# Seven of 28 pieces of the pooling of x folded by TensorE in the three steps without expert tiles

## The reference

```python
pooled = x.reshape(B, C, 14, 16, 14, 16).sum(axis=(3, 5))      # sums over 16x16 patches: 196 tokens an image
h = einsum('bcij,ce->bije', pooled, channel_weights)            # width 192
# attention, 12 heads of 16, weights 1 + qk + qk^2/2, relu, normalised by their sum
h = h + attention(layernorm(h)) @ w_proj + b_proj
# mixture of 8 experts (192 -> 768 -> 192, gelu), the best 2 of a softmax router, weighted
h = h + experts(layernorm(h))
```

## Time and profile before

| | us |
|---|---|
| runs | 1414.0, 1405.11, 1417.02; median 1414.0 |
| the profiled execution, its time | 1408.19 |
| its span, first to last instruction | 1406.3 |
| TensorE busy | 1232.2 (88%) |
| VectorE busy | 953.2 (68%) |
| sums of x (L1071), 448 of them | 358.2 |
| mean granted clock of TensorE | 0.935 of full |

### The profile page before, as it was taken

How to read it: one execution, slowest core, us unless ns; L and a number is a source line. 1 busy time by engine, 2 the same in 40 slices (tenths; PEclk the granted TensorE clock), 3 DMA queues, 4 the chain that set the end, 5 groups by cost and what they waited for, 6 DMA issues and landing times.

```text
span 1406.3 us, 26911 instructions
## 1 busy us (share of the span) xinstructions
PE 1232.2 (88%) x7299; PEld 1091.8 (78%) x7299; DVE 953.2 (68%) x3405; ACT 593.2 (42%) x1127; POOL 603.5 (43%) x485
## 2 busy tenths in 40 slices
PE   4766766789898989898989898989899889999986
PEld 3755655678787878788888888888888778888875
DVE  6799988487878787878787878787846223333444
ACT  0221224254544444444444444444444434454554
POOL 0004435414545445454545454545464553353332
PEclk9985557899999999999999999999999989999999
DMA  8679878568787878787878787777544654454554
GB/s 298 244 254 351 307 249 272 185 188 254 208 255 203 259 199 255 208 249 213 246 218 245 216 247 216 242 221 240 126 112 82 204 102 92 92 100 86 114 131 105
DMA packets 126505, 284.42 MB, mean 202 GB/s; under 512 B 24773, under 2 KB 70454, under 8 KB 126454
## 3 DMA queue, kind: packets, MB, share of 16 engines
q1 hardware_dynamic: 83350, 242.56, 52.3%
q0 software_dynamic: 43104, 41.25, 17.0%
HBM read 228.79 MB, written 54.95 MB: 202 GB/s over the span
## 4 chain that ended last, share of the span: by engine, by line
PE 28%; DMA 23%; POOL 17%; issue 15%; DVE 14%; ACT 2%; SPq 2%; POOLq 1%; DVEq 0%; ACTq 0%
DMA result<-ys,ridx 12%; PE ps L996 11%; PE ps L965 9%; POOL rows_d L616 9%; DMA rows_d<-rows,sloti 8%; POOL result L631 8%; DVE red L1071 5%; PE ps L805 2%; DMA w1r<-L_ffn_w 1%; PE ps L912 1%; DVE stats L1199 1%; DMA xr<-rows_d 1%; PE ps L1026 1%; SPq L484 1%; DVE topi L1208 1%
## 5 line engine op out<-in xcount | busy, mean ns | idle before, releaser
L631 POOL DMA_INDIRECT result<-ys,ridx x210 | 334.7, 1594 | 341.7 <-issue 189.8
L996 PE MATMUL ps<-w2a,hid 128*128 x2520 | 452.3, 327 | 1.8 <-ACT hid L730 1.8
L616 POOL DMA_INDIRECT rows_d<-rows,sloti x256 | 256.8, 1003 | 434.0 <-DMA rows_d<-rows,sloti 132.2
L996 PEld LDWEIGHTS ps<-w2a,hid 128*128 128x128 f32 x2520 | 415.2, 191 | 12.8 <-issue 3.0
L1071 DVE TENSOR_REDUCE red<-xbuf 128x21 f32<-128x672 f32 x448 | 358.2, 840 | 9.0 <-DMA xbuf<-x 8.0
L730 ACT ACTIVATE hid<-ps,b1s 128x512 f32<-128x512 f32 (+1 forms) x344 | 222.5, 653 | 264.2 <-PE ps L965 214.3
L965 PE MATMUL ps<-xh,w1h 128*128 128x512 f32 (+1 forms) x344 | 157.8, 459 | 21.7 <-ACT hid L730 8.1
L1308 DVE TENSOR_TENSOR xl<-ps,xh 128x512 fp32r<-128x512 f32 (+1 forms) x58 | 37.2, 641 | 200.8 <-ACT xh L749 200.8
L1331 DVE TENSOR_TENSOR w1l<-w1r,w1h 128x768 fp32r<-128x768 f32 x114 | 107.6, 949 | 45.8 <-ACT w1h L742 45.5
L965 PE MATMUL ps<-xl,w1h 128*128 128x512 f32 (+1 forms) x344 | 133.4, 388 | 0.0
L965 PE MATMUL ps<-xh,w1l 128*128 128x512 f32 (+1 forms) x344 | 133.3, 387 | 0.0
(11 more groups left out here) (165 smaller groups left out, 1584.3 us busy)
## 6 DMA issues: line engine op xcount, KB each, us to landing
xbuf<-x SPq DMA_DIRECT2D x224, 672.0 KB, 6.2
w1r<-L_ffn_w SPq DMA_DIRECT2D x118, 384.0 KB, 4.2
xr<-rows_d SPq DMA_DIRECT2D x48, 402.0 KB, 3.8
result<-h1s SPq DMA_DIRECT2D x32, 294.0 KB
w2a<-L_ffn_w SPq DMA_DIRECT2D x8, 576.0 KB, 7.2
rows_d<-rows,sloti POOLq DMA_INDIRECT x256
rows_d<-pad SPq DMA_DIRECT2D x9, 402.0 KB, 3.9
result<-ys,ridx POOLq DMA_INDIRECT x210
```

What stands on the lines that cost most here:

```text
L616: pool.indirect_dma_start(rows_d, bass.IndirectOffsetOnAxis(ap=sloti[:, k * NT + t:k * NT + t + 1], axis=0), rows[:, t, :], None).then_inc ...
L631: pool.indirect_dma_start(out, bass.IndirectOffsetOnAxis(ap=ridx[:, b, n:n + 1], axis=0), ys[:, b, n, :], None, compute_op=ALU.add).then_i ...
L996: last = mm(yout(g, b, n), hid[:, m % 3, cols], w, start=False, stop=m == MC - 1 and n % 2 == 1)
```

## The change

In steps 1, 2 and 3 the first seven half pieces are not summed by VectorE from `xbuf`. A new name `K.0` to `K.6` on TensorE multiplies each by the identity in four products of 128 x 168, one for each quarter (8 columns) of its 21 groups of 32, all accumulated in the same 168 columns of PSUM, three half pieces to a bank (banks 3, 4 and 5, unused in these steps). VectorE's `P` for these then sums 21 x 8 elements from PSUM; it waits for a whole bank of folded pieces at a time (`s_fold`): pieces 0 to 2 after `K.2`, 3 to 5 after `K.5`, 6 after `K.6`. The count `s_pooled`, which lets SyncE load the next chunks, is raised by VectorE as before. `K.0` to `K.4` stand ahead of `S3`, `K.5` and `K.6` between `S3` and `S4`. In steps 1 and 2 the names `P` are spread in another way: 16 instead of 18 stand ahead of `S6.0`, and one each behind `S6.0` and `S6.3` more. `LAST` keeps its places of `P`. The scatters' groups of six are as they were.

```diff
-STEP_ALONE = """S3 P P P P P P P P P P P P P P P P S4 S5 P P S6.0 S6.1 P S6.2 P S6.3 S7.0 P P S7.1 P P S8.0 P S8.1 P S8.2 P P S8.3
-    T1 S10 T2 R V.0 V.1 S11 V.2 V.3 S9 Q0 Q1 Q2 Q3""".split()
+STEP_ALONE = """K.0 K.1 K.2 K.3 K.4 S3 K.5 K.6 P P P P P P P P P P P P P P P S4 S5 P S6.0 P S6.1 P S6.2 P S6.3 P S7.0 P P S7.1 P P
+    S8.0 P S8.1 P S8.2 P P S8.3 T1 S10 T2 R V.0 V.1 S11 V.2 V.3 S9 Q0 Q1 Q2 Q3""".split()
-LAST = """S3 P P P P P P P P P P S4 S5 P P P G0 S6.0 S6.1 S6.2 S6.3 S7.0 P S7.1 P G4 P P S8.0 S8.1 S8.2 S8.3 S10
+LAST = """K.0 K.1 K.2 K.3 K.4 S3 K.5 K.6 P P P P P P P P P P S4 S5 P P P G0 S6.0 S6.1 S6.2 S6.3 S7.0 P S7.1 P G4 P P S8.0 S8.1 S8.2 S8.3 S10
...
+FOLDED = 7
+FOLD = EIGHTH // 4
...
+        s_fold = sem("pieces_folded")
...
+        def folded(p):
+
+            return ps[:, 3 + p // 3, p % 3 * SUMS * FOLD:(p % 3 + 1) * SUMS * FOLD].rearrange("q (n w) -> q n w", w=FOLD)
...
             lone[0] = not with_tiles and not last
+            by_pe[0] = not with_tiles
...
+            pe.sem_inc(s_fold, FOLDED)
+
+            def K(s, p):
+
+                k, h = p // HALVES, p % HALVES
+                pe.wait_ge(d_x[k % XSLOTS], (s + 1) * (16 * CHUNKS // XSLOTS) + 16 * (k // XSLOTS) + 16)
+                pe.wait_ge(s_pooled, s * PARTS + FOLDED)
+                for w in range(0, EIGHTH, FOLD):
+                    last = mm(folded(p), ident, xbuf[:, k % XSLOTS, h, :, w:w + FOLD], start=w == 0,
+                              stop=w == EIGHTH - FOLD)
+                last.then_inc(s_fold, 1)
...
             def P(s, p, first=False):
...
                 if p == 0 and not first:
                     dve.wait_ge(s_mix, s + 1)
-                if h == 0:
+                if by_pe[0] and after_first(s) and p < FOLDED:
+                    dve.wait_ge(s_fold, s * FOLDED + min(p // 3 * 3 + 3, FOLDED))
+                    V.tensor_reduce(red[:, p * SUMS:(p + 1) * SUMS], folded(p), AX.X, ALU.add).then_inc(s_pooled, 1)
+                    return
+                if h == 0 or p == FOLDED:
                     dve.wait_ge(d_x[k % XSLOTS], (s + 1) * (16 * CHUNKS // XSLOTS) + 16 * (k // XSLOTS) + 16)
```

More of the change, by code:

```diff
@@ L369, in vit_layer @@
         at_end = [False]
-        rank_bank, lone = [2], [False]
+        rank_bank, lone, by_pe = [2], [False], [False]
         def groups(j):
@@ L1037, in T1 @@
                 S1(s + 1)
-            schedule(pe, {"S1": S1, "T1": T1, "S3": later(S3), "S4": later(S4), "S5": S5, "S6": S6, "S7": S7, "S8": S8,
+            schedule(pe, {"S1": S1, "T1": T1, "K": later(K), "S3": later(S3), "S4": later(S4), "S5": S5, "S6": S6, "S7": S7, "S8": S8,
                           "S9": S9, "M": M, "X": X, "N": N, "G2": G2, "G3": G3})
```

## The result

Over 22 runs each, the changed kernel takes 1409.22 us (median; 1402.87 to 1414.56), the kernel before 1413.38 (1405.11 to 1421.65): a ratio of 0.9967, 95% interval 0.9953 to 0.9981, so 4.2 to 4.7 us faster. That is real and small: 0.3%. The profiled execution takes 1409.34 us, its span is 1407.5, its mean granted clock 0.939. The profile of before was a low draw of its kernel (1408.19), so the two spans can't be subtracted; I compare the lone steps inside them, of which before has this one trace. A run more than 1.5% above the fastest of its kernel counts as slow and stays out of the ratios: that takes away nine of the twelve runs of a variant further down (e5), its profiled one among them, and 13 of the 25 of the kernel before beside e1 to e4, so those ratios carry little and the medians of all runs stand beside them.

The account below looks back on a forecast made before the run. VectorE's sums of x were taken to bound steps 1 and 2, scatters and the w1 load step 3. Terms -1.3 and -2.6 made -3.9 us: 1407 from the mean, 1410 from the median, stated as 1408; range 1398 to 1420.

Parts of the forecast that it names:

- (c): Rival, whole kernel: the shift is absorbed by later scatters or waiting tiles, no effect, 1411 us; chance 0.18.
- (d): Rival, lone steps: full saving, S3 hardly late or step 3's idle time gone too, 7.8 less, 1403 us; chance 0.10.
- The work: Each lone step: 56 matrix instructions on TensorE, 0.14 us each at full clock; VectorE's short sums cost 0.26 us each.
- The clock: TensorE during K: low at the start, rising 4.1 us after K starts, between 2.7 and 5.4.
- (a): Rival, TensorE: the low clock holds through K and beyond, +21 us, 1432; chance 0.10.
- (b): Rival, TensorE: the clock rises late, at about 12 us, +2 us a step, 1415; chance 0.12.
- S3 late: TensorE: K.0 to K.4 ahead of S3 make it start 3.3 us late (2.8 to 4.0).
- The head: VectorE's sums ahead of S6: it comes for S6 at 114.2 instead of 117.29, 3.1 us earlier.
- The moved sums: Steps 1 and 2: two sums move behind S6, 1.53 us, idle time takes most of them, costing +0.5 us.
- The wait for the scatters: At S11 in step 1: step 0's scatters are through at about 141.7, so the step gives 1.3 us, not 2.6.
- Step 2: Its wait for scatters has 4.8 us to spare, so it gives 2.6 us.
- Step 3: Bound by scatters and the load of w1; its sums save nothing of their own.

Follow-up runs that it names:

- e5: The changed kernel with all of K moved behind T1 of the step before; median 1513.5 us (kernel before 1512.4), ratio 0.9923.
- e1: The kernel before with only the new places of P in steps 1 and 2; median 1511.7 us (kernel before 1509.7), ratio 1.0072.
- e4: The changed kernel without K in step 3; median 1510.5 us (kernel before 1509.7), ratio 1.0083.
- c1: The changed kernel again, no edit, on a faster chip; median 1404.8 us (kernel before 1415.3), ratio 0.9932.
- e2: The changed kernel with K run but VectorE still summing the long pieces; median 1509.0 us (kernel before 1509.7), ratio 1.0042.
- c0: The changed kernel again, no edit, on a slower chip; median 1512.6 us (kernel before 1512.4), ratio 0.9987.
- e9: The changed kernel with K.0 to K.2 behind T1 of the step before, and unused products filling two gaps; median 1411.8 us (kernel before 1415.3), ratio 0.9979.
- e3: The changed kernel with each product of K issued twice; median 1543.3 us (kernel before 1509.7), ratio 1.0270.
- e8: The changed kernel with three unused products in each gap before and after S5, steps 1 and 2; median 1408.2 us (kernel before 1415.3), ratio 0.9957.

## Why the prediction was right

The forecast was 1408, with -3.9 us as the sum; measured were 1409.22 and -4.2. Step by step:

- **The number.** The ratio's interval is -2.7 to -6.6 us. It holds the forecast's -3.9 and leaves out rivals (c), nothing, and (d), -7.8. That the level came out at 1408 as well is partly luck, since four runs with a spread of 12 us stood behind it.
- **The work.** 56 matrix instructions a step, in 7.80 + 2.47 us; the prediction had 7.65 + 2.24. At the full clock 16 take 2.40 from start to start, 0.15 each (0.14 predicted). Short sums take 0.33, 0.24 from start to start (0.33, 0.26).
- **The clock.** It rose 3.8 us after K began (2.7 to 5.4 predicted, 4.1 taken), in c1 at 99.9, 4.9 after. In all traces in which K stands ahead of S3 and begins at the low clock, 21 steps, it took 2.7 us (e2, step 2) to 5.3 (c0, step 3). The stay at the low clock, rival (a), and the late rise, (b), are out. By the Trainium skill, "TensorE: Matmul & The Clock Gate", Part 4, a transpose by the identity (in TensorE's transpose mode) does not count as activity. A plain product with the identity does, as these windows show. The Trainium skill, "TensorE: Matmul & The Clock Gate", Part 1, says that the number of products before the rise varies between executions of one kernel. The 3.8 and 4.9 us agree: 13 instructions of K had begun in the one, 17 in the other.
- **S3 late.** It starts 100.16 - 92.53 = 7.63 us after the ranking's end instead of 4.36: 3.3 late, as predicted. VectorE idles ahead of its fourth and its seventh sum (1.54, 0.33), as predicted.
- **The head.** -2.9 us in step 1 for -3.1 predicted, -3.4 in step 2. The step that I had wrong without harm: I took the clock as full through S6's first pair (113.2 against VectorE's 114.2, a margin of 1.0). It fell before S6, the pair took 1.69, and the margin was gone: TensorE came 0.1 after VectorE. In c0 and c1 the fall came before S5 and the gain shrank to 0.6 or 0.7 in one step each. So the right sum rests on a clock that falls late enough, and its range should have held that case: it is worth +2 us a step.
- **The moved sums.** I took +0.5 a step, since idle time should take most of them. Of the 1.01 us of idle time before, 0.84 are still there (0.26 and 0.58). From the first reciprocal to S11 step 1 takes 27.45 us instead of 25.70, 1.75 more; 0.26 of them are the wait at S11, so that 1.5 of the 1.53 stayed. In step 2, before idles twice:

```profile
169.33 0.36 DVE L1199 BATCH_NORM_STATS2 stats<-h1s 98x6 f32<-98x192 f32 x1 [1.02 <-ACT h1s L708]
171.78 0.36 DVE L1199 BATCH_NORM_STATS2 stats<-h1s 98x6 f32<-98x192 f32 x1 [0.95 <-ACT h1s L708]
```

  and from reciprocal to S11 it lost only 0.46 (27.16 for 26.70).
- **The wait for the scatters.** It is there (0.26 at 139.50) and ends 5.8 us after step 0's last scatter is issued at 133.71; I had 6.2, with an end at 141.7 for which the rows give only the last packets before 141. Step 1 gained 1.23 for the 1.3 of the cap. But the forecast had VectorE wait 1.3 there and it waited 0.26; what kept step 1 at 1.2 was mostly the moved sums. Two terms were off against each other: the right number came partly by the wrong one, and that is luck.
- **Step 2** gave 2.57 for 2.6, again by other parts: the head 3.4 shorter, from reciprocal to S11 0.46 longer, and VectorE's first sum 0.4 later against the scatters. **Step 3** gave 0.49 for 0. The first scatter of step 2 is at 183.06; with the 2.3 us added by which the setup was shorter it is 185.4 (185.3 predicted).
- **The rivals in the other runs.** Rival (c), nothing, is outside c1's interval too. c0's, 0.9949 to 1.0026, is wide enough to hold both (c) and the forecast. Rival (d), the full saving of 7.8, is against the distances, -4.3 in the first trace and 124.15 - 127.64 = -3.5 in c1; but c1's ratio, 0.9932 (4 runs against 19), would be -9.6 us, and its interval meets those of c0 and of the 22 runs at their ends only. Where the other 5 us of these four runs come from stays open; no distance in the lone steps shows them.

## What to carry to other kernels

Before work is moved to an idle engine, ask what else its idle time decides: here the added products, 10.0 us of them, filled 7.2 us of idle time and shortened the stages behind them by 5.2 with the clock that they raised, while the same products done earlier (e5, e9) left TensorE waiting for ScalarE, and the clock low behind that wait. When a change brings two engines level, as VectorE and TensorE at S6 here, more work on the one comes out in the time (e3: +8.6 us for +7.8), and small variations of a clock show at once. An effect of 0.3% in a kernel whose executions spread by 1% is read from distances within the changed part, not from two spans.

## What the runs showed of the hardware

- The granted clock falls in a stretch of small products with pauses of 0.92 and 0.98 us between them, in some steps ahead of S5 and in others ahead of S6, for the same code in one execution (c1, steps 1 and 2). With six dense matrix instructions in each, 1.1 us, it held in both steps of e8, and fell in the same execution's third step, which had no fillings.
- Six filling instructions take 1.1 us at the full clock and 2.0 at the low one: a filling that is free in the one case delays in the other (e9).
- S6, nearly gapless products on 91 rows, kept the low clock for all its 5.76 us in steps 1 and 2 of the kernel before, the changed kernel, c0 and c1. In e9, where the fillings left no gap from S4 on, the clock rose while S6 ran, 13.2 us after S4 began in step 1. K on 128 rows, where it stands ahead of S3 and begins at the low clock, was followed by the rise within 2.7 to 5.3 us in all 21 steps.
- The same kernel takes 1410 us on some chips and 1510 on others: the tile steps take 71.8 and 80.3 us (the change, c0), the three lone steps together 123.4 and 128.6. ScalarE's stalls of some 2 us and more were seen on the slower chips only.
